# Part of three shared expert chunks computed in the last rounds of the attention

## The reference, cut to what matters

```
logits = xn @ w_router.T              # xn: layer norm of x, 1024 tokens x 256
scores = sigmoid(logits); top 2 of 8 experts per token, weights normalised
out  = sum over the 2 chosen e:  w[e] * (silu(xn @ wg[e].T) * (xn @ wu[e].T)) @ wd[e].T
out += sum over 2 shared j:      (silu(xn @ sg[j].T) * (xn @ su[j].T)) @ sd[j].T      # 640 hidden each
```

## Time and profile before

| | us |
|---|---|
| median of three runs | 856.86 |
| lowest and highest run | 853.4, 857.02 |
| span of the profiled execution | 859.4 (no separate device time is listed for it) |
| PE busy | 775.1 (90% of the span) |
| DVE, ACT, POOL busy | 554.2, 384.4, 238.3 |

### The profile page before, as it was taken

The page is one execution under the profiler, slowest core; times in us unless marked ns, Lnnn a source line. Parts: engine busy times, 40 slices in busy tenths (PEclk is TensorE's granted clock), DMA queues, the critical chain, the costliest instruction groups (busy, mean ns, idle before and its releaser), DMA issues. The chain is left out here.

```text
span 859.4 us, 15356 instructions
## 1 busy us (share of the span) xinstructions
PE 775.1 (90%) x5288; PEld 566.7 (66%) x5288; DVE 554.2 (64%) x1291; ACT 384.4 (45%) x847; POOL 238.3 (28%) x296
## 2 busy tenths in 40 slices
PE   6899878999999999997778999989989888999995
PEld 2455546878998999993335655555555537888884
DVE  3799946533432222223987999899996357888854
ACT  2466534332321111110334766666675407888860
POOL 2344420520000000004641433444431421434340
PEclk8999988999999999999899999899999798999999
DMA  9465441390289999836610001010125119999817
GB/s 337 176 245 223 189 153 56 94 405 16 78 296 387 388 345 316 304 137 158 203 34 2 25 11 45 25 51 31 46 82 208 56 42 347 411 396 393 336 56 251
DMA packets 57104, 158.03 MB, mean 184 GB/s; under 512 B 7180, under 2 KB 36748, under 8 KB 51708
## 3 DMA queue, kind: packets, MB, share of 16 engines
q1 hardware_dynamic: 51700, 141.97, 45.5%
q0 software_dynamic: 5328, 15.08, 4.9%
HBM read 114.21 MB, written 42.81 MB: 183 GB/s over the span
## 5 line engine op out<-in xcount | busy, mean ns | idle before, releaser
L1271 PEld LDWEIGHTS ps<-f_xT,f_rg 128*128 128x128 f32 x920 | 113.4, 192 | 5.2 <-DMA f_rg<-w_routed 1.7
L1271 PE MATMUL ps<-f_xT,f_rg 128*128 128x128 f32 x920 | 113.9, 275 | 1.3 <-DMA f_rg<-w_routed 1.3
L1176 DVE TENSOR_TENSOR f_rhT<-f_gate,ps 128x256 f32<-128x256 f32 (+1 forms) x69 | 25.9, 376 | 117.2 <-ACT f_gate L981 73.0
L2078 ACT ACTIVATE b_PX<-ps 128x512 f32<-128x512 f32 x128 | 72.7, 597 | 46.3 <-PE ps L2313 44.7
L1811 DVE TENSOR_REDUCE b_smax<-ps 128x4 f32<-128x1024 f32 x64 | 77.9, 1217 | 15.7 <-PE ps L2289 15.4
L981 ACT ACTIVATE f_gate<-ps 128x256 f32<-128x256 f32 (+1 forms) x69 | 24.0, 348 | 134.2 <-PE ps L1271 134.2
L2606 POOL DMA_INDIRECT y<-f_ys,f_to x47 | 45.1, 959 | 81.7 <-DVE f_to L2684 78.2
L1285 PE MATMUL ps<-f_rd,f_rhT 128*128 128x256 f32 x230 | 62.3, 387 | 0.0
L2313 PE MATMUL ps<-b_Q,b_Cx 100*128 100x256 f32 x256 | 55.8, 327 | 6.3 <-ACT b_PX L2078 6.0
L2313 PEld LDWEIGHTS ps<-b_Q,b_Cx 100*128 100x128 f32 x256 | 41.9, 206 | 26.6 <-ACT b_PX L2078 12.2
L1583 POOL MEMSET b_half<- 128x1 f32 x1 | 0.1, 99 | 212.9 <-POOLq L69 212.9
(11 more groups left out here) (333 smaller groups left out, 1843.1 us busy)
## 6 DMA issues: line engine op xcount, KB each, us to landing
f_rg<-w_routed SPq DMA_DIRECT2D x23, 1280.0 KB
rows<-a_blank SPq DMA_DIRECT2D x16, 1152.0 KB, 7.0
f_rd<-w_routed SPq DMA_DIRECT2D x23, 640.0 KB, 5.5
f_rw<-w_ffn SPq DMA_DIRECT2D x19, 704.0 KB
rw<-w_ffn SPq DMA_DIRECT2D x16, 704.0 KB
later<-w_ffn SPq DMA_DIRECT2D x12, 704.0 KB
f_xs<-rows SPq DMA_DIRECT2D x31, 144.0 KB
f_yk<-y SPq DMA_DIRECT2D x8, 512.0 KB, 7.8
```

The source lines that it names most:

```text
L1271: mm = nc.tensor.matmul(ps[:, u % 4, k * P:(k + 1) * P], rg[b % R_SLOTS][:, off:off + P], xT[b % 2][:, c, :], start=(c == 0), stop=(c == C ...
L2078: nc.scalar.activation(PX[g % RING][:].rearrange("p c m -> p (c m)"), ps[:, RETS + G_TURN[g] % 2, :], ACT.Exp, scale=XSC).then_inc(turn_re ...
```

## The change

Gate and up of the first three chunks, for the first 512 tokens, are computed in rounds 6 to 8 of the attention, in the place of the filler matmuls; all four first chunks are split there. The order of the units becomes (0,0), (1,0), (2,0), (0,1), (1,1), (2,1), (3,0), (3,1), and so on (chunk, half). Buffers and semaphores of the units are allocated ahead of the attention. The two first `raw` loads are issued in the SP step of tile 6, the two others in that of tile 7, each ahead of two of the stores that clear DRAM regions. In `routed_experts` the unit loops begin at unit 2 (ACT, DVE) and 3 (PE); the six matmuls at the start go; DVE's routing pieces stand at later units; a weight buffer's split waits for the last `down` of the chunk before. `unit_part(u, n)` is gate (n = 0) or up (n = 1) of unit u: 6 matmuls.

```diff
@@ attention0, SP
             for t in range(2, TILES):
                 sp.wait_ge(read_out, t - 1)
                 load_ctx(t)
+                if t >= TILES - 2:
+                    for n in range(2):
+                        n += 2 * (t - TILES + 2)
+                        sp.dma_start(raw[n][:], w_shared[n]).then_inc(w_shared_loaded[n], 16)
                 for r in range(2 * t, 2 * t + 2):
                     clear_region(r)
-            for n in range(W_SLOTS0):
-                sp.dma_start(raw[n][:], w_shared[n]).then_inc(w_shared_loaded[n], 16)
@@ attention0, DVE, order of a round
                 rope(e_)
+                if b_ == TILES - 1:
+                    for j in range(1, 4):
+                        low_w(j)
                 x_shift(b_)
+                if c_ == TILES - 1:
+                    times_up(0)
+                    times_up(1)
+                    low_h(0)
                 low_part(c_)
+                if a_ == TILES - 1:
+                    low_w(0)
@@ attention0, ACT, order of a round
                 apply_norm(c_, 2)
+                if c_ == TILES - 1:
+                    high_h(0)
...
                 keep_logits(c_)
+                if a_ == TILES - 1:
+                    high_w(0)
...
                 keep_aT(a_)
+                if a_ == TILES - 1:
+                    for j in range(1, 4):
+                        high_w(j)
+                if b_ == TILES - 1:
+                    silu(0)
+                    silu(1)
@@ attention0, PE
+            def unit_part(u, n):
+                if u == 0 and n == 0:
+                    pe.wait_ge(x_added, TILES - 1)
+                    pe.wait_ge(aT_ready, TILES - 1)
+                    pe.wait_ge(low_ready, TILES // 2)
+                if u == 1 and n == 1:
+                    pe.wait_ge(x_added, TILES)
+                if u >= 2:
+                    pe.wait_ge(signals["h_ready"], u - 1)
+                pe.wait_ge(signals["wl_ready"], u + 1)
...
                 project(e_)
+                if c_ == TILES - 1:
+                    unit_part(1, 1)
+                    unit_part(2, 0)
                 turn_xn(c_, 2)
                 turn_xn(b_, 1)
                 route(c_)
+                if c_ == TILES - 1:
+                    unit_part(2, 1)
                 x_score(b_)
                 if b_ == TILES - 1:
-                    keep_busy(6)
+                    unit_part(1, 0)
...
-                if b_ == TILES - 1:
-                    keep_busy(1)
                 weigh_values(a_)
                 x_read_out(b_)
-                if b_ == TILES - 1:
-                    keep_busy(10)
                 project_out(a_)
                 turn_xn(f_, 0)
                 if a_ == TILES - 1:
-                    keep_busy(7)
-            keep_busy(4)
+                    unit_part(0, 0)
+                    unit_part(0, 1)
@@ routed_experts, ACT
-            split(0)
             act.wait_ge(clamped, 1)
             nc.scalar.activation(scores[:], logits[:], ACT.Exp, scale=-1.0).then_inc(sig_ready, 1)
-            for j in range(1, LEAD):
-                split(j)
-            for u in range(UNITS):
+            for u in range(EARLY0 - 1, UNITS):
@@ routed_experts, DVE (times_up is unit_times_up; zeros are set ahead of the clamp)
+            for u in range(EARLY0 - 1, UNITS):
+                if u == UNITS - 1:
+                    low_h(u - 1)
+                unit_times_up(u)
+                if u < UNITS - 1:
+                    low_h(u - 1)
+                if u in SPLIT_AT:
+                    split(SPLIT_AT[u])
+                at = u - EARLY0 + 1
+                if at == 0:
+                    compare()
+                    choose()
+                if at == 2:
+                    keep_counts()
+                    count_blocks()
+                if at == 3:
+                    place_rows()
+                if at == 4:
+                    combine()
+                    block_experts()
+                if 5 <= at < 5 + TOP0:
+                    locate(at - 5)
@@ routed_experts, PE (clear(t): the two zeroing matmuls of acc for half t)
             pe.wait_ge(zeros_set, 1)
-            for _ in range(6):
-                nc.tensor.matmul(ps[:, 3, :], zeros[:, 0:P], zeros[:], start=True, stop=True)
-            for u in range(UNITS):
+            clear(0)
+            for u in range(EARLY0 - LAG):
+                down(u)
+            for u in range(EARLY0, UNITS):
                 gate_up(u)
-                if u == LAG - 1:
+                if u == EARLY0 + 1:
                     count_rows()
-                if u == LAG:
+                if u == EARLY0 + LAG:
                     pe.wait_ge(counts_kept, 1)
+                    clear(1)
                 if u == UNITS - 1:
                     turn_x(0)
-                if u >= LAG:
-                    down(u - LAG)
+                down(u - LAG)
```

More of the change, by code:

```diff
@@ L40 @@
 W_SLOTS0 = 4
+H_SLOTS0 = 4
+EARLY0 = 3
 WC0 = 2 * C * P + D
@@ L63, with shared_units @@
 W_ALL = 656
+def shared_units():
+    early = [(j, 0) for j in range(EARLY0)]
+    late = [(j, 1) for j in range(EARLY0)]
+    return early + late + [(j, t) for j in range(EARLY0, SHARED_CHUNKS) for t in range(HALVES)]
 def end_program(nc, semaphores):
@@ L245, in attention0 @@
         SPAN = range(-3, TILES + 2)
+        wh, wl, act_out, h, hh, hl = (unit[n] for n in ("wh", "wl", "act", "h", "hh", "hl"))
         def tiles(n):
@@ L571, in keep_logits, with high_w, silu, high_h @@
                 nc.scalar.copy(logits[:, t, :], side(t % 2)[:, 0:E0]).then_inc(logits_kept, 1)
+            def high_w(j):
+                act.wait_ge(w_shared_loaded[j], 16)
+                nc.scalar.copy(wh[j][:], raw[j][:]).then_inc(signals["wh_ready"], 1)
+            def silu(u):
+                act.wait_ge(signals["gate_ready"], u + 1)
+                nc.scalar.activation(act_out[u % 2][:], ps[:, 2 * (u % 2), :], ACT.Silu).then_inc(signals["silu_ready"], 1)
+            def high_h(u):
+                act.wait_ge(signals["h_ready"], u + 1)
+                nc.scalar.copy(hh[u][:], h[u][:]).then_inc(signals["hh_ready"], 1)
             act.wait_ge(bufs_set, 1)
@@ L732, in route @@
                 mm.then_inc(logits_ready, 1)
+            def unit_part(u, n):
[8 more added lines that the diff above has]
+                pe.wait_ge(signals["wl_ready"], u + 1)
+                for c in range(C):
+                    at = slice((n * C + c) * P, (n * C + c + 1) * P)
+                    dst = ps[:, 2 * (u % 2) + n, :]
+                    nc.tensor.matmul(dst, wh[u][:, at], xh[:, c, 0:HT], start=(c == 0), stop=False)
+                    nc.tensor.matmul(dst, wh[u][:, at], xl[:, c, 0:HT], start=False, stop=False)
+                    mm = nc.tensor.matmul(dst, wl[u][:, at], xh[:, c, 0:HT], start=False, stop=(c == C - 1))
+                mm.then_inc(signals[("gate_ready", "up_ready")[n]], 1)
             def keep_busy(n):
@@ L770, in _ @@
                 if a_ == TILES - 1:
-                    keep_busy(7)
-            keep_busy(4)
+                    unit_part(0, 0)
+                    unit_part(0, 1)
     end_program(nc, semaphores)
 def routed_experts(nc, tag, w_shared, w_routed, rows_dram, y_dram, X, XN, xh, xl, K, KR, ps, logits, dest, wk, raw, w_loaded,
-                   ctx_rows, ctx_dram, blank_ctx):
+                   unit, signals, ctx_rows, ctx_dram, blank_ctx):
     ctx = ExitStack()
[L781 to L784, removed]
+    semaphores = list(w_loaded) + list(signals.values())
+    ORDER = shared_units()
+    UNITS = len(ORDER)
+    LAST = {j: max(u for u, (k, _) in enumerate(ORDER) if k == j) for j in range(SHARED_CHUNKS)}
+    LAG = 2
+    SPLIT_AT = {LAST[j - W_SLOTS0] + LAG + 1: j for j in range(W_SLOTS0, SHARED_CHUNKS)}
+    W_SLOTS, H_SLOTS = W_SLOTS0, H_SLOTS0
     GU = 2 * C * P
@@ L992, in _ @@
                 nc.scalar.activation(act_out[u % 2][:], ps[:, 2 * (u % 2), :], ACT.Silu).then_inc(silu_ready, 1)
-                if u >= 1:
-                    high_h(u - 1)
-                if u % HALVES == 0 and u // HALVES + LEAD < SHARED_CHUNKS:
-                    split(u // HALVES + LEAD)
+                high_h(u - 1)
+                if u in SPLIT_AT:
+                    split(SPLIT_AT[u])
             high_h(UNITS - 1)
@@ L1120, in locate, with unit_times_up @@
                     ins.then_inc(slots_ready, 1)
-            nc.vector.tensor_scalar(logits[:], logits[:], -88.7, None, ALU.max).then_inc(clamped, 1)
-            nc.vector.memset(zeros[:], 0.0).then_inc(zeros_set, 1)
-            split(0)
-            nc.vector.tensor_copy(upper[:], KR[:, R_UP:R_UP + P])
-            sigmoid()
-            compare()
-            split(1)
-            choose()
-            for u in range(UNITS):
-                if u == UNITS - 1:
-                    low_h(u - 1)
+            def unit_times_up(u):
                 dve.wait_ge(up_ready, u + 1)
@@ L1225, in down @@
             def down(u):
```

(2 more changed lines are left out.)

78 lines of the change are left out of this document (41 added, 37 removed).

## The result

The changed kernel takes 847.16 us (median of 4 runs, 846.42 to 848.82) where the kernel before takes 856.94 us beside it (853.4 to 859.52). The ratio is 0.9879, 95% interval 0.9848 to 0.9911: 9.8 us less, where 7.65 were forecast. The profiled run of after took 847.1 us with a span of 845.2, against a span of 859.4 before.

What follows compares the result with a forecast made beforehand. PE, never resting in the shared units, was taken as the bound there. 8.4 + 2.3 - 1.4 - 0.95 - 0.7 = 7.65 us off the 859.4 us span gave 851.7, a median of 849.2 us; range 844.5 to 853.8.

Steps and rivals of the forecast that it cites:

- Shared phase: Shared units on PE: three units' gate and up leave, 36 matmuls at 0.233 us, a gain of 8.4 us.
- Start of the section: After the attention's barrier: six unused matmuls leave, wait before real work falls from 3.8 to 1.5 us, gain 2.3 us.
- POOL's norm: Attention, tile 7: two POOL norm instructions meet DVE's subtractions, 0.7 us longer each, cost 1.4 us; bounds 0 and 1.9.
- The tail: End of the attention: unit 2's halves wait for silu(0) and delay PE's end, cost 0.95 us; bounds 0.9 and 1.5.
- The clock: Around the barrier: PE's clock falls near 131.25 and returns near 138.05 as before, net -0.7 us; +1.2 if it stays up.
- Loads at 0: Attention: the four chunks' loads, issued one and two rounds earlier, cost 0; upper bound 4.7 us if they land late.
- Table loads hidden: Start of the next section: ACT's two more table loads hide behind PE's 20 matmuls (4.65 us), 0.5 us to spare.
- The scatter: Shared phase: POOL's last piece comes 7 us later, near 164.5; SP reaches the row loads at 191.6, 19 us left.
- rival 5: Shared phase: scatter stores and row loads stretch over 19 us, PE stands still; 860 us at 30; chance 0.03.
- rival 4: Routed blocks: they end when their DMA loads end, so the gain is hidden anyway; 856.9 us; chance 0.05.
- Rival 1: Attention's end and barrier: POOL undisturbed and clock up, gain 10.9 us, 846.0 us; chance 0.20.
- signs named: Included PE's last attention matmul near 133.5 to 134.9, six table loads, last shared down near 217, unchanged distance to the end.

Runs made afterwards that it cites:

- e1: Kernel before with the shared chunks' buffers (wh, wl, act, h, hh, hl) allocated ahead of the attention, no instruction changed: 856.28 us, ratio 0.9974.
- e10: Kernel before with only wh and wl moved to their addresses in the changed kernel, no instruction changed: 854.95 us, ratio 0.9969.
- e11: Changed kernel with an 8224-byte pad per partition, putting the units' buffers back at the addresses of before: 848.07 us, ratio 0.9873.
- e2: Kernel before without the six unused matmuls at the start of the shared phase: 857.56 us, ratio 0.9994.
- e3: Changed kernel with VectorE's low parts of chunks 1 and 2 behind GpSimd's tile 7 norm, chunk 3's behind the softmax: 845.29 us, ratio 0.9837.
- e4: Changed kernel with two units instead of three in the attention, the third's gate and up left in the section: 850.01 us, ratio 0.9914.
- e5: Kernel before with eight more filler matmuls in the attention's last round: 856.46 us, ratio 0.9979.
- e6: Changed kernel with the first four chunks' loads in their old place, behind the last round's clearing stores: 848.55 us, ratio 0.9899.
- e7: Changed kernel with an unused small Silu and Exp behind the scores' Exp, so two more table loads: 853.38 us, ratio 0.9929.
- e13: Changed kernel again, nothing edited, run beside e10 to e12: 847.78 us, ratio 0.9865.
- e8: Kernel before with two 32-byte pads per partition, shifting only the units' buffers from 0 to 32 modulo 64 bytes: 858.33 us, ratio 1.0004.
- e12: e3 with unit 2's silu in the attention, its h and unit 1's halves first in the section, its up before the last route: 845.11 us, ratio 0.9857.

## Why the prediction was right, step by step

- **Shared phase, 8.4 us.** The mechanism held: PE was never idle before, so matmuls taken out were time gained, and the routed phase kept its length (162.07, 161.84). What was missing is a term: the pitch. 17 units of 12 and 20 of 6 matmuls are 324, by 0.0059 us 1.9 us. The prediction carried 0.233 us over from rows 2, a figure that held for the old addresses only; e1, e10 and e11 show that it changes with the addresses of the buffers.
- **Start of the section, 2.3 us.** Measured 2.0 (3.88 to 1.84 us; 3.8 to 1.5 was said, where 134.95 is the start of the last filler and real work starts at 135.02). The words "the six unused matmuls leave too" made the gain look like theirs; e2 shows that their removal alone gives no gain that can be seen, since PE then waits for the split.
- **POOL's norm, -1.4 us.** Right, and mis-sized by little: 1.19 and 1.28 us for 0.55 and 0.26, +1.66 us, towards the upper bound of 1.9. e3 is its undoing and gives 1.3 back. The Trainium skill (GPSIMD Engine Reference, Key points) names the contention with VectorE instructions of two SBUF inputs; the trace agrees, with 0.64 and 1.02 us.
- **The tail, -0.95 us.** 1.1: the last tile's transpose 0.5 later, and 0.6 more from it to PE's end. `unit_part(2, 0)` waited for `h` of unit 0 exactly as worked out.
- **The clock, -0.7 us.** This step failed. "The holes become other holes, not fewer" was wrong: the clock stayed at 1.00 through the barrier, so that 1.5 us came in, less the stall of 0.27 us, in place of -0.7: the step was off by 1.9 us. e4, with one unit fewer, has the half clock back at 134.98, and e5, with more fillers in the same tail, has it too. What in the real ones keeps it up was not separated: e5's fillers have another type (bf16 zeros) and do not stand in the same holes as the third unit's matmuls. Nor is the size fixed: the 1.5 us is what this one profile of before loses, and e1 and e10, with the same fillers, lose only some 0.25.
- **Loads at 0.** Right in the changed place; e6 shows that in the old place there is a stall, of 2.7 us where the bound was 4.7.
- **Table loads hidden, with 0.5 us to spare.** Hidden, and `hl` of unit 2 came late once as said, with 0.27 us lost at 147.23 for 0.35. But the spare was 0.15 us, not 0.5. The 20 matmuls cover the time until `down` of unit 1, which needs `hl` of unit 1, and VectorE makes that behind the `h` of unit 2 with which the prediction ended its count. That each us beyond the cover costs one was wrong too: e7 lost about twice that in the trace, since the clock fell in the wait. Six loads as counted, each 1.28 us. By the Trainium skill (ScalarE: Activation LUTs, What ACT_TABLE_LOAD costs) a drain of some 1380 ns belongs to a switch; the loads at 128.83 and 138.74 have their silu right behind them, and e7's at 140.26 and 141.77 begin where the activation ahead of them ends, so the traces contradict it here as rows 9 did.
- **The scatter.** The row loads were issued from 191.95 (191.6 was said), and `turn_x` at 209.02 waited for nothing: rival 5 did not occur, nor rival 4.

Rival 1, all goes well (846.0), came nearer in time than the forecast (849.2; measured 847.16), but in part for another reason: its clock was right and its undisturbed POOL wrong, and the pitch filled the difference. The terms as measured, 8.4 + 1.9 + 2.0 - 1.66 - 1.1 + 1.5 - 0.3, are 10.7 us; the medians gave 9.8 and, beside e13, 11.3. So two terms of nearly 2 us each, the clock and the pitch, were missed on the same side. The forecast of 7.65 lies nearer to the medians (2.1 us) than to its own terms as measured (3.1 us), and that is luck.

Of the signs named, the six table loads, the longer POOL instructions, the real matmuls and the unchanged routed phase came. PE's last matmul in the attention ended at 136.0, outside the 133.5 to 134.9 that was named, and the last shared `down` came at 214.94, not near 217. The first has a reason outside the change: the attention is another 2.2 us longer in the profile of after by slow stretches of the clock (1.2 up to 107.3, and 1.0 from there to tile 7's norm). The second part is 13.97 us long in after and in e1, whose attention is that of before, and 13.01 in before with its shorter slow stretch. So chunk 0's split and the earlier loads cost nothing there, as predicted, and neither this nor the gap of 0.9 in before is counted.

## What to carry to other kernels

Where one engine is never idle, count what leaves it, then ask which wait the unused instructions were covering: taking out those alone gave nothing that could be seen. Work pulled into the holes ahead of a barrier can pay twice, once as work and once by the clock that stays up, and a new wait can cost twice for the same reason, as the one of 2.89 us in e7 did. What one profile loses to the clock can be the luck of that profile: look at the clock of several runs with the same instructions before counting it. When buffers move, compare the durations of untouched instructions first: a few ns on 300 matmuls are as much as one of the edits.

## What the hardware showed that was not expected

- The same matmul (128 rows, 512 columns, fp32r) runs at another pitch at full clock by where the buffers lie in SBUF. Gate and up, with `xh` at byte 36320 of a partition, take 0.2267 us where `wh` starts at 65248 (e1, after) and 0.2335 where it starts at 73472 (before, e11), and by 32 bytes more it is still 0.2333 (e8). `down` takes 0.231 with all buffers at the old place, 0.234 where only its weights have moved (e10), and 0.2267 where all have (e1). Which distance or which bits decide stays open.
- Two GpSimd instructions on one column took 1.19 and 1.28 us, for 0.55 and 0.26, while VectorE ran three subtractions of 768 columns; 0.55 and 0.27 again when the subtractions stood behind them (e3).
- A wait of 2.89 us on PE was followed by 6 us at 1.2 GHz instead of 2.4 (e7); the changed kernel's waits of 1.84 and 0.63 us were not followed by a fall. A barrier with 1.70 us without a matmul came with a fall behind filler matmuls (before, e1, e5, e8, e10), one of 2.10 us with a fall behind two units (e4), and ones of 1.61 to 1.84 us with none behind three units (after, e3, e6, e7, e11, e12, e13).
